# One-hot tiles of an edge count built eight at a time, and the edge scatters started from half of their slots

## What is computed

```
xn = layernorm(x)
h = xn @ W
norm = deg_inv_sqrt[src] * deg_inv_sqrt[dst]
gnn = segment_sum(h[src] * norm[:, None], dst)         # 20,625 edges given, 625 self loops added
q, k, v = heads(xn @ W_qkv)
q1 = exp(q' - diag(q) - max over features) + eps       # q' = q @ proj_mat.T, scaled
k1 = exp(k' - diag(k) - max over ALL nodes and heads) + eps
mix = (q1 @ (k1.T @ v)) / (q1 @ sum(k1)) @ W_proj + b
x = x + gnn + mix
x = x + experts(layernorm(x))                          # top 3 of 15, and one shared
```

## Time and profile before

| | |
|---|---|
| Median of 3 runs | 1267.51 us (1267.04 to 1268.6) |
| The profiled execution: its own time | 1266.61 us |
| Its span, first to last instruction | 1264.9 us |
| Busy: PE, DVE, ACT, POOL | 1146.0, 788.2, 660.2, 499.5 us |
| Mean granted TensorE clock | 0.961 of full speed |

### The profile page before, as it was taken

How to read it: one execution, slowest core, us unless ns; L and a number is a source line. 1 busy time by engine, 2 the same in 40 slices (tenths; PEclk the granted TensorE clock), 3 DMA queues, 4 the chain that set the end, 5 groups by cost and what they waited for, 6 DMA issues and landing times.

```text
span 1264.9 us, 20941 instructions
## 1 busy us (share of the span) xinstructions
PE 1146.0 (91%) x6438; PEld 1006.5 (80%) x6439; DVE 788.2 (62%) x1478; ACT 660.2 (52%) x1042; POOL 499.5 (39%) x351
## 2 busy tenths in 40 slices
PE   2999946999549899999999999999999999999985
PEld 1999946887435557888889998888999888899974
DVE  7832613256399584662586597465596698655983
ACT  4122617236210303443687668566677796676863
POOL 1078877888630050026232243121343272323421
PEclk9899977999879899999999999999999999999998
DMA  9030000550110012212678666647657887386943
GB/s 311 1 84 2 2 2 2 138 172 6 15 75 2 1 58 92 88 25 55 219 263 321 225 210 241 201 149 280 214 205 282 306 321 229 134 307 215 347 164 96
DMA packets 62948, 191.72 MB, mean 152 GB/s; under 512 B 14172, under 2 KB 15239, under 8 KB 62902
## 3 DMA queue, kind: packets, MB, share of 16 engines
q1 hardware_dynamic: 50134, 172.52, 37.2%
q0 software_dynamic: 11728, 18.27, 8.2%
q10 hardware_dynamic: 1040, 0.33, 0.1%
HBM read 178.74 MB, written 15.09 MB: 153 GB/s over the span
## 4 chain that ended last, share of the span: by engine, by line
PE 58%; POOL 17%; DVE 10%; issue 7%; DMA 3%; ACT 2%; ACTq 0%; SPq 0%; DVEq 0%; POOLq 0%
PE banks L1910 23%; PE banks L1894 22%; POOL edge_dram L721 17%; PE banks L1832 3%; DVE ohd L966 3%; PE banks L1878 2%; DVE ohs L965 2%; PE banks L1882 2%; PE banks L1804 2%; DMA out<-ysb,sidx 2%; PE banks L1871 1%; PE banks L1652 1%; DVE w2lo L525 1%; DMA xs<-in_x 1%; DMA xn_dram<-xn 1%
## 5 line engine op out<-in xcount | busy, mean ns | idle before, releaser
L721 POOL DMA_INDIRECT edge_dram<-epair,eslot x165 | 216.1, 1310 | 111.1 <-DVE eslot L936 61.4
L800 POOL DMA_INDIRECT out<-ysb,sidx x27 | 118.8, 4399 | 237.1 <-issue 205.8
L512 ACT ACTIVATE w2hi<-w2raw 128x1536 fp32r<-128x1536 f32 x96 | 139.2, 1483 | 90.4 <-DMA w2raw<-in_L_ffn_fc_w 78.9
L525 DVE TENSOR_TENSOR w2lo<-w2raw,w2hi 128x1536 fp32r<-128x1536 f32 x96 | 164.3, 1752 | 22.9 <-ACT w2hi L512 20.7
L1910 PE MATMUL banks<-w2hi,hthi 128*128 128x384 f32 x624 | 161.4, 339 | 0.0
L1910 PE MATMUL banks<-w2lo,hthi 128*128 128x384 f32 x624 | 159.1, 335 | 0.0
L1910 PE MATMUL banks<-w2hi,htlo 128*128 128x384 f32 x624 | 158.9, 335 | 0.0
L512 ACT ACTIVATE w1hi<-w1raw 128x1536 fp32r<-128x1536 f32 x96 | 137.2, 1495 | 27.3 <-DMA w1raw<-in_L_ffn_fc_w 24.7
L525 DVE TENSOR_TENSOR w1lo<-w1raw,w1hi 128x1536 fp32r<-128x1536 f32 x80 | 147.7, 1910 | 0.2 <-DVE xs L1128 0.2
L1894 PE MATMUL banks<-w1hi,xthi 128*128 128x512 f32 x486 | 139.7, 396 | 3.0 <-POOL w1lo L525 3.0
L1894 PE MATMUL banks<-w1lo,xthi 128*128 128x512 f32 x486 | 136.8, 390 | 0.0
(11 more groups left out here) (338 smaller groups left out, 1956.3 us busy)
## 6 DMA issues: line engine op xcount, KB each, us to landing
w1raw<-in_L_ffn_fc_w SPq DMA_DIRECT2D x96, 768.0 KB, 6.6
w2raw<-in_L_ffn_fc_w SPq DMA_DIRECT2D x96, 768.0 KB, 6.1
xs<-in_x SPq DMA_DIRECT2D x10, 336.0 KB
edge_dram<-epair,eslot POOLq DMA_INDIRECT x165, 2.6
wg<-in_L_gnn_W SPq DMA_DIRECT2D x1, 2304.0 KB, 13.7
wv<-in_L_mix_W_qkv SPq DMA_DIRECT2D x1, 2304.0 KB, 20.1
wk<-in_L_mix_W_qkv SPq DMA_DIRECT2D x1, 2304.0 KB, 24.2
wq<-in_L_mix_W_qkv SPq DMA_DIRECT2D x1, 2304.0 KB, 10.8
```

Of the source, the lines that this page charges most:

```text
L512: act.activation(unit(w2hi if second else w1hi, second, u), unit(w2raw if second else w1raw, second, u), ACT.Copy).then_inc(w2_hi if secon ...
L525: eng.tensor_tensor(unit(w2lo if second else w1lo, second, u), unit(w2raw if second else w1raw, second, u), unit(w2hi if second else w1hi, ...
L721: pool.indirect_dma_start(out=edge_dram, out_offset=bass.IndirectOffsetOnAxis(ap=eslot[:, k:k + 1], axis=0), in_=epair[:, k, :].bitcast(I3 ...
L800: pool.indirect_dma_start(out=out, out_offset=bass.IndirectOffsetOnAxis(ap=sidx[:, 0:1], axis=0), in_=ysb[:, :], in_offset=None, bounds_ch ...
```

## The change

1. **One-hots in batches.** `oh` holds five batches of eight tiles, with the source and the destination one-hot as the innermost pair: `[128, RING, BATCH, TP, 2]`. One `tensor_tensor` compares `iota_r` (the index, each value twice) with `ecode` (the table in fp16), both broadcast, and writes 2,000 elements in each partition. 24 batches stand for 370 operations. PE reads both operands of a count at a step of two elements.
2. **Place of the counts.** No one-hots within attention. Parts 0 and 1 of the projection run without counts; the counts lie beside parts 2 to 7, after every second step. Part 1 uses bank 6. The part between the counts and the degree sum is part 8 where it was 7, so one part is left behind the degree sum, not two; the matmuls of messages wait for each tile of `hs` and not for all.
3. **Edge slots in two halves** of 82 and 83 columns (`slots_of`), the first before and the second after the low half of `v`; POOL starts scatters after the first. The scans are cut at bucket 8, and the ranks are taken after the second row group of `h`. `wq` is loaded after the second half.
4. **Key maximum** at scatter 62; `nbias` before the first square of `q` and the last weight split. ACT interleaves the key exponentials and the columns of `q` in finer steps. The ones column goes to DVE.
5. **Front.** DVE normalises tiles 1 and 3 of `xn`, ACT the other three; the low half of `h`'s weights comes before the last two pieces of `xlo`.

```diff
-RING = 48
+BATCH, RING = 8, 5
-ONES_AT, MAX_AT = 16, 76
+MAX_AT = 62
+HALVES_OF_EDGES = [(0, ET // 2), (ET // 2, ET)]
...
+FIRST_BESIDE, LAST_BESIDE = 2, 8
...
+def beside(n, third):
+
+    return ET_TILES * (3 * (n - FIRST_BESIDE) + third) // (3 * (LAST_BESIDE - FIRST_BESIDE))
...
-            groups([("pj", n // 2, n % 2)], [0 if n == 2 * NT - 2 else 7])
-            if n == 2 * NT - 3:
+            groups([("pj", n // 2, n % 2)], [6 if n == 1 else 0 if n == 2 * NT - 1 else 7])
+            if n == 2 * NT - 2:
...
-            pool.wait_ge(eslot_ok, 1)
             pool.wait_ge(st_epad, 16)
             for k in range(ET):
-                if k == ONES_AT:
-                    done(pool, ("h", NT - 1, 1))
-                    pool.memset(vext[:, :, :, HD:HD + 1], 1.0).then_inc(vones_ok, 1)
+                for n, (a, b) in enumerate(HALVES_OF_EDGES):
+                    if k == a:
+                        pool.wait_ge(eslot_ok, n + 1)
...
-                    dve.tensor_scalar(ohs[:, t % RING, 0:TP], iota_n[:, :], etab[:, t, 0:1], None, ALU.is_equal)
-                    dve.tensor_scalar(ohd[:, t % RING, 0:TP], iota_n[:, :], etab[:, t, 1:2], None, ALU.is_equal).then_inc(oh_ready, 1)
+            def one_hots(n):
+
+                if n >= RING:
+                    dve.wait_ge(oh_free, n - RING + 1)
+                dve.tensor_tensor(oh[:, n % RING, :, :, :], iota_r[:, :, :].unsqueeze(1).broadcast_to([128, BATCH, TP, 2]),
+                                  ecode[:, BATCH * n:BATCH * n + BATCH, :].unsqueeze(2).broadcast_to([128, BATCH, TP, 2]),
+                                  ALU.is_equal).then_inc(oh_ready, 1)
...
+            dve.wait_ge(norm_ok, 1)
+            for i in (1, 3):
+                dve.tensor_scalar(xn[:, i, :], xs[:, i, :], lnrs[:, 3, i:i + 1], lnrs[:, 4, i:i + 1], ALU.mult, ALU.add).then_inc(xn_dve, 1)
             dve.wait_ge(const_ok, 1)
-            link(run(0, BUCKETS // 2))
-            for n, (kind, k) in enumerate(T8):
+            link(run(0, 8))
+            for kind, k in T8[:C]:
                 x_lower(kind, k)
             split_low(dve, "h", 0)
-            link(run(BUCKETS // 2, BUCKETS))
+            for kind, k in T8[C:]:
+                x_lower(kind, k)
+            link(run(8, BUCKETS))
             bucket_totals()
             split_low(dve, "h", 1)
             edge_slots()
+            slots_of(*HALVES_OF_EDGES[0])
             split_low(dve, "v", 0)
+            slots_of(*HALVES_OF_EDGES[1])
...
-            split_low(dve, "q", 1)
-            square("q", 0)
             squares_to(("sqk", 0), 0)
             dve.wait_ge(kall_ok, 1)
...
+            square("q", 0)
+            split_low(dve, "q", 1)
...
+            dve.tensor_copy(ecode[:, 0:ET_TILES, :], etab[:, :, :]).then_inc(iota_r_ok, 1)
+            dve.wait_ge(iota_r_ok, 2)
+            for batch in range(RING):
+                one_hots(batch)
+            for n in range(FIRST_BESIDE):
+                add_projection(n // 2, n % 2)
...
-            rows_times("h", {2: bucket_ranks})
+            rows_times("h", {1: bucket_ranks})
...
+                    made = oh[:, t // BATCH % RING, t % BATCH, :, :]
+                    last = pe.matmul(banks[0:TP, bass.ds(where[t % OFFSETS], TP)], made[:, :, 0], made[:, :, 1],
...
+                if n == FIRST_BESIDE:
+                    counts_begin()
...
-            project_out(2 * NT - 2)
             project_out(2 * NT - 1)
-            pe.wait_ge(h_scaled, NT)
```

More of the change, by code:

```diff
@@ L450, in taken, with turn_tokens @@
             eng.wait_ge(free[b], n)
-        def turn_tokens(pe, name, rows, ready, per_tile, after=lambda n: None):
-            for n, (kind, k) in enumerate(T8):
+        def turn_tokens(pe, name, rows, ready):
+            for kind, k in T8:
                 ps = fill(pe, (name, kind, k))
@@ L918, in edge_slots, with slots_of @@
                 link(dve.tensor_tensor(efrom[0:TP, 1:BUCKETS], efrom[0:TP, 1:BUCKETS], elast[:, 0:BUCKETS - 1], ALU.subtract))
-                for b in range(BUCKETS):
-                    last = dve.scalar_tensor_tensor(out=epos[:, b, :], in0=erun[:, b, :], scalar=efrom[0:TP, b:b + 1], in1=ehot[:, b, :],
+            def slots_of(a, b):
+                for n in range(BUCKETS):
+                    last = dve.scalar_tensor_tensor(out=epos[:, n, a:b], in0=erun[:, n, a:b], scalar=efrom[0:TP, n:n + 1], in1=ehot[:, n, a:b],
@@ L1358, in _ @@
             act.wait_ge(norm_ok, 1)
-            for i in range(NT):
+            for i in (0, 2, 4):
                 act.wait_ge(ld_x[i], 32)
@@ L1385, in take_rows, with take_columns @@
                 emptied(ins, (name, i, s))
-            def take_columns(name, o):
-                for s, (a, b) in enumerate(TSPLIT):
+            def take_columns(name, o, parts=(0, 1)):
+                for s in parts:
+                    a, b = TSPLIT[s]
                     ps = read(act, (name, o, s))
@@ L1618, in _ @@
             filled(last, ("lt", 0))
-            all_turned(pe, "xt")
+            for kind, k in T8[:C]:
+                taken(pe, ("xt", kind, k))
             def half_square(name, o, i):
@@ L1768, in _, with counts_begin @@
             pe.wait_ge(const_ok, 3)
-            turn_tokens(pe, "at", ao, const_ok, 0)
+            turn_tokens(pe, "at", ao, lambda i: None)
             all_turned(pe, "at")
             pe.wait_ge(ld_wp, 16)
-            pe.wait_ge(ld_offs, 16)
-            pe.wait_ge(eye_ok, 2)
-            for n in range(COUNT_BANKS):
-                width = min(4, BUCKETS - 4 * n) * TP
-                own = [j for j in range(4) if (4 * n + j) % (NT + 1) == 0 and 4 * n + j < BUCKETS]
-                a = TP * (4 - own[0]) if own else 0
-                pe.matmul(bank[n][0:TP, 0:width], eye[:, 4 * TP:5 * TP], eye[:, a:a + width], start=True, stop=False,
-                          skip_group_check=True)
+            def counts_begin():
+                pe.wait_ge(ld_offs, 16)
+                pe.wait_ge(eye_ok, 2)
+                taken(pe, ("pj", 0, 1))
+                for n in range(COUNT_BANKS):
+                    width = min(4, BUCKETS - 4 * n) * TP
+                    own = [j for j in range(4) if (4 * n + j) % (NT + 1) == 0 and 4 * n + j < BUCKETS]
+                    a = TP * (4 - own[0]) if own else 0
+                    pe.matmul(bank[n][0:TP, 0:width], eye[:, 4 * TP:5 * TP], eye[:, a:a + width], start=True, stop=False,
+                              skip_group_check=True)
             where = []
@@ L1807, in project_out @@
                         filled(last, ("pj", i, s))
-                    m = C * n + c
-                    if m < TILES_BESIDE:
-                        count(ET_TILES * m // TILES_BESIDE, ET_TILES * (m + 1) // TILES_BESIDE)
-            for n in range(2 * NT - 2):
+                    if FIRST_BESIDE <= n < LAST_BESIDE and c % 2:
+                        count(beside(n, c // 2), beside(n, c // 2 + 1))
+            for n in range(2 * NT - 1):
                 project_out(n)
```

120 lines of the change are left out of this document (62 added, 58 removed).

## The result

The changed kernel takes 1235.97 us, median of 4 runs (1235.49 to 1237.68), against 1267.28 (1266.83 to 1268.6) for the kernel before, run in turn with it: a ratio of 0.9754, 95% interval 0.9737 to 0.9771, or 31 us less. The prediction was 1235. The profiled execution took 1235.79, its span is 1234.1.

The account below looks back on a forecast made before the run. The chain through edge slots, scatters and one-hots to the messages' start at 444.5 us bounds it; -30.1 to the counts' end and -2.2 behind make -32.3 from 1266.61: 1234.3, or 1235 as median; forecast 1229 to 1240, wider range 1225 to 1248.

Parts of the forecast that it names:

- Part 1: Up to the first scatter: ranks asked earlier -5.0, slots in halves -6.6; first scatter at 54.6 us, against 66.2.
- Part 2: Chain of scatters: second half of slots beside it costs 3.0 us (0 to 7.5); last starts at 328.5, against 337.4.
- Rival C: GpSimd loses more to VectorE: second slot half 7.5, bias adds 10.7, together 6.2 us more, 1241; chance 0.09.
- Part 3: Key maximum earlier: `nbias` at 163.5, attention ending 31 us earlier near 303; only slack, none of it in the sum.
- Part 4: Table to counts: five batches 5.6 us, two adds 1.1, bias adds 9; TensorE gets projection part 2 at 349.7.
- rival A: One-hot batches run at one element a cycle: five cost 5.2 us more, VectorE's pace 6.9 more, 1247; chance 0.12.
- bias term: GpSimd's bias adds beside VectorE's batches, ahead of the counts: 9 us lost, between bounds of 3.6 and 10.7.
- Part 5: Counts beside six projection parts: 37.5 us, plus identity matmuls 2.0 and lower clock 1.6; counts end at 390.8, against 420.9.
- Rival B: Counts slow down because TensorE reads operands at a step of two: 11 us at most, 1246; chance 0.06.
- Part 6: Degree sum to first expert: one part fewer saves 3.9, TensorE waits 2.4; 2.2 us shorter, between 0 and 3.9.

Follow-up runs that it names:

- runs at 76 and 92: Changed kernel with the key maximum's all-reduce ahead of scatter 76 or 92 and not 62: 1232.2 us (ratio 0.9730) and 1255.1 us (0.9906).
- first profile: Profiled execution of the changed kernel in its first set of runs: 1235.79 us, span 1234.1; set median 1235.97 us.
- second profile: The changed kernel itself, nothing altered, profiled again with a later set of five runs: span 1230.2 us; set median 1233.7 us, ratio 0.9725.

## Why the prediction was right, point by point

**Part 1, first scatter (54.6):** right in sum and in its terms. Forecast -6.6 for the half of the slots, measured -7.5 by the kernel that takes it back. `etiles` came 5.1 earlier, for -5.0.

**Part 2, the chain (+3.0 for the second half):** mis-sized. Forecast 328.5 for the last start, measured 325.3; the term was next to nothing, its lower bound. Scatters do take longer beside long VectorE operations (2.17 to 3.32 us beside the early splits of 2.5), as the prediction had read, but the 25 operations last 0.22 us each, and the three scatters beside them took 1.33, 1.21 and 1.22. Rival C's 7.5 is refuted: the whole chain took 270.9 us. The Trainium skill (SBUF — State Buffer, SBUF: two separate sides) has a VectorE operation with two SBUF inputs and a GpSimd operation that reads SBUF shut each other out for a whole instruction. Whether the issue of an indirect DMA is such an operation no run here isolates; the waits seen are not longer than the operations beside them, 1.0 to 2.1 us beside the splits and under 0.2 beside the short ones.

**Part 3, the key maximum:** `nbias` at 161.18 against 163.5, attention's end at 302.7 against 303, and the worth of nothing by itself. The runs at 76 and 92 show both: 21 us later costs nothing, 45 us later costs 19 to 21. Measured slack is some 26 us.

**Part 4, batches and bias sums:** 1.196 us a batch against 1.19; rival A (2.24) is what the kernel without the inner pair does. The bias term was mis-sized: 9 taken, 4.9 measured, near the lower bound of 3.6. Its mechanism was misread too. It took the 7.21 us of the earlier trace rows for a wait for a gap in the one-hots, but GpSimd stands still as long (7.06 us) where VectorE has no one-hots to build. This time the pause covered the five batches, so the sums had next to nothing to collide with once they ran, and the loss was VectorE's wait for the first tile. That the term came out small is luck of the timing; the forecast did not see it. TensorE began at 342.55, part 2 at 345.18; forecast for the former was 349.7.

**Part 5, six parts (6.25 each):** mis-sized. They took 42.2 us from 345.18 to the end of the counts, 7.0 each. The loads of offsets were in no term, though the kernel before has loads too; eight of the 12 cost 4.0 us together. Rival B is refuted by 0.059 us a count. The lower clock cost 2.6 us in the identity matmuls and the first four of the projection (against the kernel with the maximum at 92), where 1.6 was forecast; without it the identity matmuls take 1.35 to the next start, against 2.0.

**Part 6 (-2.2):** the step that failed in the first profile. The two terms shown for it, 3.9 saved and 2.4 waited, would give -1.5 and not -2.2. From the end of the counts to the first expert matmul it took 58.5 us against 56.6 before, +1.9; in the second profile 55.8, -0.8. The wait for the third message was forecast at 2.4 and is 4.01 and 2.35. The rest is the clock, whose lower stretches fall on the part ahead of the messages and on the messages in one and not in the other. In both the third message starts 17.2 us behind the first, when VectorE has done its splits, so the wait is only as long as the messages before it are quick. The forecast's 2.4 was right in kind and the term still 1.4 to 4.1 too good.

So that the total came within 1 us is partly luck, a sum of errors of both signs: -3.2 from the scatters, -4.0 from the bias sums and batches, +3.7 from the counts with what stands ahead of them (44.8 us from 342.55 against 41.1), +1.4 to +4.1 from part 6. Where the time came from is as forecast within 4 us a stretch: 12.1 up to the last scatter (forecast 8.9), 22.6 from there until TensorE goes on (39.8 before, 17.2 now; forecast 18.6), and 1.1 lost in the counts (43.7 before, 44.8 now; forecast 2.6 saved).

## What to carry to other kernels

Cost a change against the point where the stretch next becomes all TensorE, and price a moved wait by the slack it makes; one constant moved twice (76, 92) gives the size of that slack. For two-byte comparisons against a broadcast value, lay the pair that differs innermost: it halved a batch. Measure a register load by itself before regrouping a loop around it: here each regrouping cost 19 to 27 us, for a reason that stays open. When an engine stands still, look for the same wait in a kernel where its supposed cause is absent, before naming the cause. And where VectorE waits for a sum that GpSimd gets to late, let VectorE make it: 3 to 4 us here.

## What the runs showed of the hardware that was not expected

- Loads of 16 offsets into TensorE's registers stopped the counts for 0.45 to 0.54 us each, eight of 12, where they start at multiples of 16 tiles; regrouped to other starts most kept TensorE waiting for 1.0 to 2.7 us and made the kernel 19 to 27 us longer. That the start is the reason is a reading of the rows and not isolated.
- Behind its scatters GpSimd stood still for 6.8 to 7.5 us ahead of its next additions, whatever VectorE did meanwhile: five batches of 1.2 us, one-hots of 0.26, or no one-hots at all (7.03, 7.21 and 7.06 us). The cause is open.
- Short VectorE operations left indirect-DMA issues beside them alone (1.21 to 1.33 us beside `SCALAR_TENSOR_TENSOR` operations of 0.22 us); the three early ones beside splits of 2.5 us took 2.17 to 3.32.
- The same instructions gave spans of 1234.1 and 1230.2 us: the stretches with a lower granted clock fall in other places from execution to execution.
